# A transformer layer with two recurrences on one core: feed-forward one batch behind attention, and a recurrence unit placed at the border of two batches

## The reference

```python
x = x + attn(cond(x, fside, fside, w1, u1, cond_512), w_qkv, w_o)
x = x + ffn(cond2(x, fside, fside, w2, u2, cond_512), w_gate, w_up, w_down)

# cond and cond2: a recurrence over time in both directions
ek = exp(min(k, 30)); ekv = ek * v          # k = v = fside
nf, df = scan(a*decay + ekv), scan(b*decay + ek)          # forward
nb, db = the same scans, reverse=True
euk = exp(min(u + k, 30))
out = sigmoid(r) * (nf + nb - ekv + euk*v) / max(df + db - ek + euk, 1e-8) * (0.8 + 0.2*tf)   # r = x

# attn: 16 heads of 32, causal softmax(q k / sqrt(32)) v, then w_o
# ffn: every linear quantises its input (6-bit elements) and its weight (4-bit) in blocks of 32
gate, up = q(x) @ q(w_gate).T, q(x) @ q(w_up).T           # 512 to 2048
out = q(silu(gate) * up) @ q(w_down).T                    # 2048 to 512
```

## Time and profile before

| | us |
|---|---|
| median of 3 runs | 970.66 |
| lowest, highest | 970.17, 975.77 |
| the profiled execution | 973.96 |
| its span, first to last instruction | 972.2 |
| TensorE busy | 783.0 |
| VectorE busy | 767.2 |
| ScalarE busy | 474.2 |

### The profile page before, as it was taken

How to read it: one execution, slowest core, us unless ns; L and a number is a source line. 1 busy time by engine, 2 the same in 40 slices (tenths; PEclk the granted TensorE clock), 3 DMA queues, 4 the chain that set the end, 5 groups by cost and what they waited for, 6 DMA issues and landing times.

```text
span 972.2 us, 10499 instructions
## 1 busy us (share of the span) xinstructions
PE 783.0 (81%) x3816; PEld 383.8 (39%) x3857; DVE 767.2 (79%) x1057; ACT 474.2 (49%) x758; POOL 74.2 (8%) x149
## 2 busy tenths in 40 slices
PE   2666537688889999798899998987899989987656
PEld 1222213345544444355444444554344444643222
DVE  2999999788996878989968798799777986524566
ACT  4756634438664362376643623666546234452230
POOL 1000000211100002111000021110000211100000
PEclk9767758899978999999879999989999999999788
DMA  8622210435300003654000036540000263300001
GB/s 319 238 64 101 88 44 11 100 97 154 94 18 16 1 11 87 184 142 109 11 22 1 11 82 189 141 108 13 23 0 11 71 189 87 88 1 1 0 1 43
DMA packets 30306, 72.25 MB, mean 74 GB/s; under 512 B 5808, under 2 KB 5808, under 8 KB 28464
## 3 DMA queue, kind: packets, MB, share of 16 engines
q1 hardware_dynamic: 19792, 46.94, 16.3%
q0 software_dynamic: 6144, 16.79, 7.3%
q10 hardware_dynamic: 4320, 7.87, 2.4%
HBM read 33.82 MB, written 4.19 MB: 39 GB/s over the span
## 4 chain that ended last, share of the span: by engine, by line
PE 55%; DVE 25%; issue 8%; ACT 7%; DMA 3%; SPq 1%; POOL 0%; DVEq 0%; ACTq 0%
PE bank L1290 11%; PE bank L1153 8%; PE bank L1146 6%; PE bank L1230 6%; PE bank L1219 5%; PE bank L1302 5%; PE bank L1203 4%; PE bank L1179 3%; ACT region L501 3%; PE bank L1204 2%; DMA stacks<-rows 2%; DVE negmax L958 2%; DVE num L858 2%; DVE fn L844 1%; PE bank L1205 1%
## 5 line engine op out<-in xcount | busy, mean ns | idle before, releaser
L958 DVE TENSOR_REDUCE negmax<-bank 128x4 f32<-128x512 f32 (+2 forms) x96 | 99.3, 1035 | 50.3 <-PE bank L1181 50.2
L1203 PE MATMUL bank<-stacks 128*128 128x512 f32 (+3 forms) x256 | 112.5, 441 | 32.8 <-ACT region L501 29.6
L501 ACT ACTIVATE region<-bank 128x512 f32<-128x512 f32 (+3 forms) x256 | 100.9, 433 | 68.6 <-PE bank L1205 68.1
L298 POOL DMA_DIRECT2D stacks<-rows x128 | 70.1, 555 | 767.6 <-DVE region L743 362.7
L1153 PE MATMUL bank<-h,wqkv 128*128 128x512 f32 x256 | 115.1, 600 | 6.7 <-DVE region L1110 4.2
L1179 PE MATMUL bank<-stacks 128*128 128x128 f32 (+3 forms) x256 | 86.8, 420 | 8.1 <-DVE negmax L958 4.4
L1203 PEld LDWEIGHTS bank<-stacks 128*128 128x128 f32 x256 | 53.5, 209 | 67.2 <-ACT region L501 51.2
L1146 PE MATMUL bank<-wqkv,h 128*128 128x512 f32 x128 | 66.4, 672 | 16.0 <-ACT rows L489 16.0
L1204 PE MATMUL bank<-maxrow,pick 128*128 128x384 bf16 (+3 forms) x236 | 79.1, 335 | 0.0
L1290 PE MATMUL bank<-region,gate_q 128*128 128x512 bf16 x244 | 60.7, 386 | 18.3 <-DVE region L743 15.5
L1153 PEld LDWEIGHTS bank<-h,wqkv 128*128 128x128 f32 x256 | 48.4, 193 | 64.8 <-issue 55.3
(11 more groups left out here) (156 smaller groups left out, 1368.7 us busy)
## 6 DMA issues: line engine op xcount, KB each, us to landing
stacks<-rows SPq DMA_DIRECT2D x128, 128.0 KB, 3.9
stacks<-rows POOLq DMA_DIRECT2D x128, 128.0 KB, 4.2
kt<-in_fside ACTq DMA_DIRECT2D x30, 256.0 KB, 3.1
h<-in_x SPq DMA_DIRECT2D x4, 1024.0 KB, 5.8
region<-in_w_gate SPq DMA_DIRECT2D x4, 1024.0 KB, 12.0
xt<-in_x SPq DMA_DIRECT2D x4, 1024.0 KB, 7.7
region<-in_w_up SPq DMA_DIRECT2D x4, 1024.0 KB, 5.6
region<-in_w_down SPq DMA_DIRECT2D x4, 1024.0 KB, 4.7
```

The lines of the kernel that those rows point to most:

```text
L298: eng.dma_start(stacks[HD * r:HD * r + HD, at:at + 2, i, :].bitcast(F32), rows[mine, q:k + 1:k - q, :]).then_inc(stacked[s][i], 16)
L501: nc.scalar.activation(probs[:, i, P_AT[t]:P_AT[t] + CAUSAL[t]], bank[4 + n % 2][:, 0:CAUSAL[t]], ACT.Exp, scale=SCALE).then_inc(p_ready, 1)
L958: nc.vector.tensor_reduce(o, scored, AX_X, ALU.max, negate=True).then_inc(max_taken, 1)
L1203: nc.tensor.matmul(o, ks[s][:, i, P * t:P * t + P], qs[s][:, i, P * t:T], start=True, stop=False)
```

## The change

- The feed-forward of batch b-1 runs in the border after the attention of batch b; that of the last batch comes alone at the end. In turn 0 there is none. The last batch's input is quantised between the gate steps of the feed-forward before it.
- The sum x2 and its tanh are written to device memory (`kept_x2`, `kept_tanh`) and read back into `xt` when needed. The input's quantisation uses scratch within `xt` (for the last batch within `v_sb`, with the ratio in `h`).
- Units: in turn b, u = 0 to 3 now belong to the second recurrence of batch b-1 (in turn 3, 4 to 7 are that of batch 3). Within attention VectorE does finish 2 and units 3 to 8; finish 9, backward 10, add 10 and forward 11 stand behind the four chunks of the rounding.
- Down weights: only the first chunk is rounded in the setup, the other three beside the attention of batch 0; ScalarE loads them again into `xt` (`down_steps`). TensorE's work on their block maxima is moved behind the projections of batch 0.
- ScalarE's `copy_raw(b, 2)` comes ahead of the reciprocals and weightings at the start of a turn.
- Scores by key: tiles 2 and 3 of a head share one bank and one exponential, 12 units for a group instead of 16. In slots 0 and 1 one mask matmul serves two heads.

The core of the diff:

```diff
+    KEY_TILES = ((0,), (1,), (2, 3))
+    PER_HEAD = len(KEY_TILES)
-    UNITS = HG * TT
+    UNITS = HG * PER_HEAD
...
+        def batch_of(b, u):
+            b, u = normal(b, u)
+            return b - 1 if u < CJ else min(b + 1, B - 1)
...
+            def x2_back(n):
+                sp.wait_ge(up_ready, (n + 1) * (FJ // 2))
+                sp.wait_ge(x2_kept, (n + 1) * (16 * CJ))
+                sp.dma_start(xt[:, :, :], kept_x2[n]).then_inc(x2_in, 16)
...
-                load_k(b, 2)
-                reciprocals(b, 2)
-                own_exp(b, 3)
-                weigh(b, 3, 0)
+                if b == 0:
+                    down_steps(1)
+                cap_exp(b, 4)
                 copy_raw(b, 2)
...
+                    load_k(b, 10)
+                    reciprocals(b, 10)
+                    own_exp(b, 11)
+                    copy_raw(b + 1, 3)
+                    weigh(b, 11, 0)
+                    weigh(b, 11, 1)
...
+                for i, c in enumerate(ROUNDING):
+                    to_fp8(ic, w, inter[:, 4 * c:4 * c + 4, :])
+                    from_fp8(ic, w, inter_q[c]).then_inc(iq_ready, 1)
+                    if i == 0:
+                        finish(b, 9)
+                    elif i == 1:
+                        backward(b, 10, 0)
+                        backward(b, 10, 1)
+                    elif i == 2:
+                        add_own(b, 10)
+                    else:
+                        forward(b, 11, 0)
+                        forward(b, 11, 1)
...
             for b in range(B):
                 turn(b, b + 1 < B)
+            feed_forward(B - 1, B)
```

More of the change, by code:

```diff
@@ L1 @@
 import math
+from collections import namedtuple
 from contextlib import ExitStack
@@ L28 @@
 KEEP_BINADE = 1.0 - 2.0 ** -9
+Scratch = namedtuple("Scratch", "top moved tile inv scale q8 xq")
 class Chain:
@@ L347, in _ @@
                 turn(b, b + 1 < B)
+            x2_back(B - 1)
+            store(B - 1)
             sp.wait_ge(weights_in, 32)
@@ L423, in load_k @@
             def load_k(b, u):
-                if live(b, u) and live(b, u + 2):
-                    act.wait_ge(summed, unit(b, u)[2] + 1)
-                    act.dma_start(kt[:, u % 2, :], fside_tile(b, u + 2)).then_inc(k_in[u % 2], 16)
+                if not live(b, u):
+                    return
+                U = unit(b, u)[2]
+                if U + 2 < 2 * CJ * B:
+                    act.wait_ge(summed, U + 1)
+                    act.dma_start(kt[:, u % 2, :], fside_tile(U + 2)).then_inc(k_in[u % 2], 16)
             def reciprocals(b, u):
@@ L703, in _ @@
                 turn(b, b + 1 < B)
+            gates(B - 1, B)
         def over(t, n=4):
@@ new lines, in top_exponents, with close_input @@
+            def top_exponents(qc, n):
+                gate, ratio, w = ffn_input(n)
+                for j in range(CJ):
+                    exponents(qc, ratio[:, j, :], w.tile if j else w.top)
+                    if j:
+                        qc.link(nc.vector.tensor_tensor(w.top, w.top, w.tile, ALU.max))
+            def close_input(qc, n):
+                gate, ratio, w = ffn_input(n)
+                from_fp8(qc, w, w.xq).then_inc(xq_ready, 1)
+                assert qc.n == QUANT_STEPS, qc.n
@@ L993, in turn @@
             def turn(b, more):
+                n = b - 1
+                qc = Chain(dve, quant, QUANT_STEPS, n)
                 maxima(b, 0, 0)
-                finish(b, 1)
+                finish(b, 2)
+                cap(b, 4)
+                if b == 0:
+                    down_sums(ch, 1)
                 maxima(b, 0, 1)
-                backward(b, 2, 0)
+                backward(b, 3, 0)
                 maxima(b, 0, 2)
-                backward(b, 2, 1)
+                backward(b, 3, 1)
@@ L1011, in turn @@
+                finish(b, 3)
+                cap(b, 5)
                 maxima(b, 1, 0)
-                backward(b, 3, 0)
+                backward(b, 4, 0)
                 maxima(b, 1, 1)
-                backward(b, 3, 1)
+                backward(b, 4, 1)
                 maxima(b, 1, 2)
-                add_own(b, 3)
+                if b == 0:
+                    down_round(ch, 2)
+                add_own(b, 4)
                 maxima(b, 1, 3)
-                forward(b, 4, 0)
+                forward(b, 5, 0)
@@ L1019, in turn @@
                 maxima(b, 1, 4)
-                forward(b, 4, 1)
                 maxima(b, 1, 5)
                 split_maxima(b, 1)
-                finish(b, 3)
-                cap(b, 5)
-                backward(b, 4, 0)
-                backward(b, 4, 1)
+                forward(b, 5, 1)
+                finish(b, 4)
+                cap(b, 6)
+                if b == 0:
+                    down_sums(ch, 3)
+                backward(b, 5, 0)
                 maxima(b, 2, 0)
-                add_own(b, 4)
+                backward(b, 5, 1)
@@ L1030, in turn @@
                 maxima(b, 2, 1)
                 normalise(b, 0)
-                forward(b, 5, 0)
+                add_own(b, 5)
+                if b == 0:
+                    down_round(ch, 3)
+                    wq_done.append(ch.n)
                 maxima(b, 2, 2)
-                forward(b, 5, 1)
-                finish(b, 4)
+                forward(b, 6, 0)
                 maxima(b, 2, 3)
-                cap(b, 6)
-                backward(b, 5, 0)
                 maxima(b, 2, 4)
-                backward(b, 5, 1)
+                forward(b, 6, 1)
@@ L1041, in turn @@
                 maxima(b, 2, 5)
                 split_maxima(b, 2)
-                add_own(b, 5)
-                forward(b, 6, 0)
-                forward(b, 6, 1)
+                finish(b, 5)
+                cap(b, 7)
+                backward(b, 6, 0)
                 maxima(b, 3, 0)
@@ L1049, in turn @@
                 maxima(b, 3, 1)
-                finish(b, 5)
-                cap(b, 7)
-                backward(b, 6, 0)
+                backward(b, 6, 1)
                 maxima(b, 3, 2)
-                backward(b, 6, 1)
+                add_own(b, 6)
                 maxima(b, 3, 3)
-                add_own(b, 6)
+                forward(b, 7, 0)
                 maxima(b, 3, 4)
-                forward(b, 7, 0)
                 maxima(b, 3, 5)
@@ L1104, in turn @@
                 finish(b, 8)
+                if b:
+                    feed_forward(n, b)
+                else:
+                    backward(b, 9, 0)
+                    backward(b, 9, 1)
+                    add_own(b, 9)
+                    forward(b, 10, 0)
+                    forward(b, 10, 1)
+                    finish(b, 9)
+                    cap(b, 11)
+                    backward(b, 10, 0)
[3 more added lines that the diff above has]
+                    forward(b, 11, 1)
```

525 lines of the change are left out of this document (319 added, 206 removed).

## The result

The changed kernel takes 986.25 us (median of 4 runs, 984.53 to 986.56), the kernel before 971.59 (4 runs, 970.17 to 975.77): a ratio of 1.0143, 95% interval 1.0113 to 1.0173. It is slower by 14 to 15 us (13.9 by the ratio, 14.7 by the medians); forecast were 952 us, range 932 to 973. The profiled execution took 984.53 us for a span of 982.8.

A forecast was written before the change was run, and what follows sets the result against it. VectorE was taken to bound setup and attention 0 to 2, TensorE the borders, both by turns the tail. Setup, attention parts and borders summed to a 953.2 us span for 972.2, scaled to 952 us, range 932 to 973.

The forecast's parts named there:

- VectorE idles 11.1 us of 109.4; I take 7 as what is left of that, 96.5 us: Attention 1 and 2: VectorE's work falls from 98.3 to 89.3 us, plus 7 idle; each part 96.5, ends 90 and 109.4.
- The floor of 90: Attention 1 and 2: least time for VectorE's 89.3 us of work and TensorE's need of 90.1 us.
- Rival (c): Attention parts: exponentials behind reciprocals in ScalarE's row pace TensorE; span 43 us longer, 994 us, chance 0.07.
- Its threshold, a mean part of 104 us: Four attention parts at a mean of 104 us come to 19 us above the forecast's 397, the whole gain.
- Attention 0 and 3: Attention 0: VectorE 105.2 us, time 111, ends 106 and 118; attention 3: VectorE some 79, time 93, ends 90 and 101.
- The copy: Head of a batch: TensorE's 4.0 us wait for ScalarE's copy goes, its own need falling from 94.1 to 90.1 us.
- Setup: Before the first scores: projection from 126.4, 3 of 14.1 us of waits kept; 167 for 191.1 us, bounds 163 and 175.
- Borders: Between attention parts: border 0 49.5 us without feed-forward; borders 1 and 2 95 for 88.8, chunks 6.1 us later.
- Last border: Last border and tail: gate/up starts at 22.3 us, then feed-forwards of 63 and 64.4; 149.7 for 93.7, ends 145 and 156.
- Rival (d): Feed-forwards: a returned load lies open in each, adding 12 to 31 us; 964 to 983 us, chance 0.05.
- Rival (a): Attention parts reach both floors, 107, 90, 90 and 90, fuller TensorE lifting the clock; 928 us, chance 0.13.

The follow-up runs named there:

- Experiment 1: Changed kernel with ScalarE's blocks of units 5 and 6 moved behind the last exponential of groups 1 and 2; 964.69 us, 0.9913 of the kernel before.
- experiment 9: Changed kernel with ScalarE's blocks of units 4 to 7 behind their groups' last exponentials and VectorE's add_own of units 5 and 6 ahead of the maxima; 955.52 us, 0.9818.
- experiment 8: Changed kernel with ScalarE's blocks of units 4 to 7 behind the last exponential of their groups 0 to 3; 957.66 us, 0.9829.
- experiment 7: Kernel before with only ScalarE's copy_raw moved ahead of the block and weighting of unit 3; 958.92 us, 0.9827.
- experiment 6: Changed kernel with all units back beside the scores, turn rows as in the kernel before, except copy_raw of group 2 early; 953.57 us, 0.9778.
- 3: Changed kernel with all units back beside the scores and ScalarE's and VectorE's turn rows as in the kernel before, copy_raw late; 963.94 us, 0.9901.
- 10: Experiment 6 with the key tiles unmerged, 16 a group instead of 12; 959.28 us, 0.9856.
- experiment 11: Experiment 6 with ScalarE's block of unit 4 behind the ninth exponential of group 1 and VectorE's finish of unit 4 later; 956.19 us, 0.9823.
- experiment 2: Changed kernel with VectorE's add_own of units 5 and 6 moved ahead of maxima and normalising, ScalarE's row as changed; 967.29 us, 0.9936.

## Why the prediction was wrong

**The step that failed** is "VectorE idles 11.1 us of 109.4; I take 7 as what is left of that, 96.5 us". I took idle time as something that shrinks with the load, from an average over the part, and charged the change's new rows of ScalarE and VectorE with nothing. The idle time grew to 17.0 us. Experiment 1 shows that these two parts were to be had at 97.4 and 100.7 us with the load as computed: the load was right, and the order was not looked at. The floor of 90 no version reached in them; the least were 96.5 us for attention 1 (experiment 9) and 96.0 for attention 2 (experiment 8). In the kernel before, the blocks of units 5 and 6 stood between two groups (455.09 and 472.32 on ScalarE), where TensorE weighs values and needs no exponential. Only the block of unit 4 stood inside group 1, and TensorE waited 1.98 us behind it (at 441.92). The change put units 5 and 6 in the middle of a group. That could be read from the diff.

**Rival (c)**, "ScalarE's order", with 994 us and a chance of 0.07, is what happened: it gave attention 1 and 2 109.4 (105.7 and 107.1), attention 3 105 (100.5), attention 0 116 (115.6). Its argument against itself, "VectorE is busy 90% of the time and ScalarE 60%", was the error: a row can hold another engine while its engine is idle 40% of the time, if its head waits for a third. My "Against it" named the busy share where the place of each wait was wanted. Its threshold, a mean part of 104 us, was also sound: the mean came to 107.2.

**Attention 0 and 3.** Attention 0: VectorE busy 103.6 (105.2 forecast), time 115.6 for 111; with the blocks of units 4 and 7 moved too, 111.5 (experiment 8), where 4.5 us of VectorE's work also left the part (busy 99.1). Attention 3: VectorE 79.15 (79), time 100.5 for 93; in no version with the feed-forward one batch behind did it come below 94.8, while 88.3 was had without the move (experiment 7).

**The copy.** The 4.0 us of the earlier trace rows were rightly seen to go, but "TensorE's own need is the 94.1 of batch 3 less the 4.0" was too small a gain: 88.3 in experiment 7, for the clock behind the wait. There the change held a gain of some 10 to 15 us (experiments 6 and 7), and lost it again, with more, to the blocks.

**Setup.** First scores at 163.4 for 167. TensorE projects from 125.34 (126.4 forecast), and of the 14.1 us of waits of the earlier trace rows one of 2.23 is left on its way to the first scores where I had kept 3. Its timeline:

```profile
125.34 9.54 PE L1312 MATMUL bank<-wqkv,h 128*128 128x512 f32 x16 [9.65 <-DVE h L996]
...
160.76 3.61 PE L1325 MATMUL bank<-rows,less_ident 128*128 128x512 f32 x4 [2.23 <-ACT rows L552]
```

**Borders.** 48.9 for 49.5, 94.3 and 94.2 for 95. VectorE's timeline of border 1 answers to the earlier trace rows, the first and last of the chunks and the last sum:

```profile
497.23 2.29 DVE L830 TENSOR_TENSOR region<-region 128x2048 fp8e4<-128x2048 f32 x1
...
517.49 2.29 DVE L830 TENSOR_TENSOR region<-region 128x2048 fp8e4<-128x2048 f32 x1
526.10 2.48 DVE L1297 TENSOR_TENSOR xt<-bank,xt 128x512 f32<-128x512 f32 x4 [0.94 <-PE bank L1499]
```

The chunks span 20.3 us for 14.2, the 6.1 us that were forecast, and TensorE waits 2.73 and 1.23 us for the last two (L836), also as forecast.

**Last border.** 153.1 for 149.7: TensorE's timeline, to set beside the earlier trace rows.

```profile
853.15 3.60 PE L1487 MATMUL bank<-xt,gate_q 128*128 128x512 bf16 x8 [9.41 <-DVE xt L836]
```

Gate/up begins 23.4 us after the start of the projection (22.3 forecast; its own terms, 13.9 + 2.5 + 5.7, come to 22.1), and the two feed-forwards take 129.7 us (127.4): after the wait of 9.41 the first eight matmuls take 3.60 us, where those of border 1 take 1.89.

**Loads.** Rival (d) did not come: no engine waits for a returned load of `xt` in the whole trace; these loads take 4.8 us (x2) and 7.0 us (the tanh) to land. The stack loads take 4.3 us in the median on both queues, for 3.9 and 4.2 before, and TensorE waits 2.55 us for one in attention 1 where it waited 0.85; no run tells the traffic's part in that from an earlier need. Rival (a) held that fuller engines lift the clock. The clock did move, but with the waits, and here it worked against the change; the earlier trace rows show that the stretch with the lower clock also had more idle time of TensorE (3.6 us for 2.5), not that gaps brought the clock down.

**Worth of the parts**, from the runs: copy_raw early -15 us (on the kernel before; -10 in experiment 6 against 3); merging -6 (experiment 6 against 10); the feed-forward's move with the roundings 0 to -5, not told apart from nothing; the unit's move in good rows +2, within the uncertainty; the rows as the change wrote them, +31 (986.25 to 955.52), of which 22 are the two blocks of groups 1 and 2 taken alone. These come from different pairs of versions and do not add up exactly. What stays open: the 2.5 us that TensorE waits in the second group for a transfer (stacks, at 370.73) were not tried, nor, with all units beside the scores, the block of unit 4 outside its group.

## What to carry to other kernels

Where engines hand work to each other through two banks, follow each in-order row and ask what stands ahead of the item that another engine waits for and what that waits for in turn; the busy share of the row's engine does not show it. When a piece of side work is moved, put it where the engine that would wait behind it has other work, here between groups, and look at whether slower matmuls follow a wait on TensorE, and count them with it. When an experiment is to take a wait away, look in its trace whether the wait went or only moved (experiment 11). Load moved from a full stage to another is worth having only after the order is right, and then it may be even.

## What the runs showed of the hardware

A wait of TensorE can cost more than its length. Behind the wait of 4.00 us the next eight matmuls took 6.36 us in batch 3 and 5.13 to 5.19 in the others, and 3.65 without the wait (experiment 7). Behind one of 4.28 us the granted clock was 0.52 over 7 us, and behind one of 1.98 us in experiment 2 too; it was as low from 345 to 352 us of the changed kernel, behind waits of only 0.74 and 1.78 us (at 343.64 and 345.81).

But not every wait is followed by the lower clock. Behind the wait of 2.55 us for a transfer (at 370.73 of the changed kernel) it was 1.00:

```profile
370.70:377.70 7.00, 6.52 (x45) 4.55 (x45) 6.03 (x8) 3.75 (x8) 0.00 (x0) 1.00 0.26 59
```

and so it was from 403 to 410 us of experiment 1, behind a wait of 1.76 us (at 402.05). What tells these cases apart, no run here shows.

The Trainium skill, "TensorE: Matmul & The Clock Gate", section "Why this matters for your kernels", asks to keep longer idle gaps out from between bursts of matmuls, to avoid throughput drops. The runs agree, and price one case: 6.7 us in all (4.00 + 2.71) for a wait of 4.00 in batch 3, and 5.5 in the other batches. Shorter waits than the section names were followed by the lower clock here too.

And a wait does not tell its price alone: in experiments 1 and 2 TensorE's idle time in attention 1 was the same within 0.3 us (14.5 and 14.8), its busy time 82.87 and 87.67 us.
